# GpSimd makes ten of the 64 drives of a selective scan: steps 11 and 27 join its list

## The reference

```python
x_proj, z = split(x @ W_in + b_in, 2)
u = silu(x_proj)                      # (8, 128, 256)
Bm, Cm = split(u @ W_x + b_x, 2)      # (8, 128, 16) each
dt = softplus(u @ W_dt + b_dt)
def step(h, inp):                     # over the tokens
    u_t, dt_t, B_t, C_t = inp
    dA = exp(dt_t[..., None] * A)
    h = h * dA + (dt_t * u_t)[..., None] * B_t[:, None, :]
    y_t = einsum('bds,bs->bd', h, C_t) + D_param * u_t
    return h, y_t
y = y * silu(z)
```

## Time and profile before

| | us |
|---|---|
| median of 3 runs | 354.48 (354.1 to 355.01) |
| the profiled execution | 354.9 |
| its span in the trace | 353.1 |
| first scan starts | 137.8 |
| last scan starts | 253.2 |

### The profile page before, as it was taken

One profiled execution on the slowest core, in us unless ns is written; L12 is line 12 of the kernel. 1 busy time (PEld: TensorE's weight loads), 2 busy tenths in 40 slices (PEclk: granted clock), 3 DMA queues, 4 the chain that ended last, 5 costly groups with the idle time before them and its releaser, 6 DMA issues.

```text
span 353.1 us, 5637 instructions
## 1 busy us (share of the span) xinstructions
PE 308.1 (87%) x1742; PEld 238.5 (68%) x1742; DVE 294.5 (83%) x743; ACT 215.0 (61%) x504; POOL 196.2 (56%) x233
## 2 busy tenths in 40 slices
PE   8759496898999999599777989898899999999993
PEld 5557395796765566464436865575798779989872
DVE  1898999997987999999999999999949446745945
ACT  4567323334164958667698548888565876756742
POOL 2599996775415062889979898979702800100111
PEclk9958599899999999879999999999999999999998
DMA  7930000000000003565645545536200000000011
GB/s 195 405 161 4 1 0 3 0 1 2 0 2 1 0 0 128 158 186 152 212 144 167 178 130 164 186 124 175 65 2 0 2 0 3 1 0 2 1 32 30
DMA packets 12853, 26.62 MB, mean 75 GB/s; under 512 B 1375, under 2 KB 2527, under 8 KB 12567
## 3 DMA queue, kind: packets, MB, share of 16 engines
q1 hardware_dynamic: 12823, 26.25, 23.2%
HBM read 25.59 MB, written 0.66 MB: 74 GB/s over the span
## 4 chain that ended last, share of the span: by engine, by line
PE 37%; DVE 16%; issue 9%; ACT 7%; POOL 7%; POOLq 0%; DVEq 0%
PE ps L1904 6%; DVE arena L772 5%; DVE ps L759 5%; POOL arena L1117 5%; PE ps L1941 4%; PE ps L1929 4%; PE ps L1930 3%; PE ps L1894 2%; PE ps L1917 2%; PE ps L1918 2%; PE ps L1858 1%; PE ps L1773 1%; PE ps L1592 1%; PE ps L1781 1%; DVE stats L476 1%
## 5 line engine op out<-in xcount | busy, mean ns | idle before, releaser
L1117 POOL TENSOR_TENSOR arena<-arena 128x512 f32<-128x512 f32 x63 | 79.3, 1273 | 21.2 <-DVE arena L772 18.5
L772 DVE TENSOR_TENSOR_SCAN arena<-arena,ps 128x512 f32<-128x512 f32 x56 | 67.0, 1208 | 0.2 <-ACT arena L1394 0.2
L1164 POOL TENSOR_TENSOR rstd<-veps,mhalf 128x4 f32<-128x4 f32 (+2 forms) x6 | 5.0, 838 | 64.4 <-DVE veps L881 35.5
L1394 ACT ACTIVATE arena<-arena,neg_a 128x508 f32<-128x508 f32 x56 | 38.2, 715 | 3.8 <-DVE arena L772 3.4
L800 DVE TENSOR_REDUCE arena<-ps 128x2 f32<-128x496 f32 x32 | 21.3, 666 | 22.6 <-PE ps L1904 22.6
L1858 PE MATMUL ps<-first_in,arena 128*128 128x128 f32 x256 | 39.0, 280 | 0.8 <-POOL arena L1117 0.8
L1858 PEld LDWEIGHTS ps<-first_in,arena 128*128 128x128 f32 x256 | 32.5, 145 | 10.3 <-issue 3.8
L759 DVE TENSOR_TENSOR ps<-arena,ps 128x512 f32<-128x512 f32 x56 | 37.9, 678 | 0.5 <-PE ps L1842 0.4
L1842 PE MATMUL ps<-arena,pick_wide 96*128 96x512 bf16 x56 | 22.0, 398 | 15.2 <-DVE arena L772 13.2
L1671 PE MATMUL ps<-arena,first_in 128*128 128x128 f32 (+1 forms) x192 | 26.7, 303 | 8.6 <-POOL arena L1004 8.6
L1671 PEld LDWEIGHTS ps<-arena,first_in 128*128 128x128 f32 x192 | 25.8, 217 | 11.3 <-POOL arena L1004 11.2
(11 more groups left out here) (291 smaller groups left out, 808.0 us busy)
## 6 DMA issues: line engine op xcount, KB each, us to landing
arena<-bc_rows_dram SPq DMA_DIRECT2D x72, 256.0 KB, 3.3
fold_in<-in_fold_dram SPq DMA_DIRECT2D x1, 2056.0 KB, 12.0
late_in<-in_late_dram SPq DMA_DIRECT2D x1, 1423.5 KB, 17.0
early_in<-in_early_dram SPq DMA_DIRECT2D x1, 921.5 KB, 13.8
xres<-in_x_dram SPq DMA_DIRECT2D x1, 512.0 KB, 14.6
kv_ctx<-in_context_dram SPq DMA_DIRECT2D x1, 480.0 KB, 8.0
rows_in<-in_rows_dram SPq DMA_DIRECT2D x1, 384.0 KB, 14.9
first_in<-in_first_dram SPq DMA_DIRECT2D x1, 320.0 KB, 5.3
```

Of the source, the lines that this page charges most:

```text
L772: nc.vector.tensor_tensor_scan(hist[:, q % NBUF], fade[:, q % NFADE], chain(q), 0.0, ALU.mult, ALU.add).then_inc(S("scan"), 1)
L1117: tt(seen[:, q % NBUF], hist[:, q % NBUF], c_wide[:, q % NBUF], ALU.mult).then_inc(S("read_out"), 1)
L1394: act(decay.rearrange("p (b t) -> p b t", t=T)[:, :, 1:], dt[:, n, cols(g)].rearrange("p (b t) -> p b t", t=T)[:, :, 1:], ACT.Exp, scale=n ...
```

## The change

Two steps are added to the list; nothing else is edited. All that hangs on the list follows from it: for steps 11 and 27 the widening on PE and the drive on DVE go; a memset on DVE, a drive on GpSimd and a broadcast in SP's queue come; the fade goes to PSUM, and its place in `FADES` moves behind the fades of the next two steps.

```diff
-        BY_POOL = (7, 15, 19, 23, 31, 44, 51, 60)
+        BY_POOL = (7, 11, 15, 19, 23, 27, 31, 44, 51, 60)
```

## The result

The changed kernel takes 358.39 us (median of 4 runs, 358.04 to 359.26), beside 354.50 for the kernel before (4 runs, 354.10 to 355.01): 1.0115 times as long, 95% interval 1.0103 to 1.0127; the medians differ by 3.9 us. 358.5 was predicted. The profiled execution took 358.56 us, its span is 356.7; before, 354.9 and 353.1.

The account below looks back on a forecast made before the run. DVE was taken to set the pace of the scan stage. The terms -0.22 + 3.90 + 0.3 gave +4.0 us, so 358.5 us; own range 357.4 to 359.4, with part of Rival 4 357.3 to 360.0.

Parts of the forecast that it names:

- Step 27: ACT, turn 24: fade 29's wait starts the long block 2.69 us later, fade 27 follows it; scan 27 3.90 us late.
- Step 11: Scan 14, held by ACT's softplus waiting for PE, comes 0.22 us earlier through the dropped widening; bounds 0 and 0.95 us.
- The clock: After PE's idle gap behind step 29's widening, half clock slows work towards scan 31: 0.3 us, bounds 0 and 1.0.
- Rival 3: ACT's block delays fade 27, but fade 29 doesn't wait: +1.21 - 0.22, 355.5 us; chance 0.05.
- Rival 1: ACT doesn't hold step 27 back; GpSimd sets the time up to drive 31: 354.1 us; chance 0.06.
- Rival 4: PE at half clock leaves DVE waiting for widened rows over several steps: 1 to 2 us more, about 360; chance 0.12.
- The broadcasts' term of 0: One 256 KB broadcast per added step in SP's queue, ahead of a row of C: 0 taken, bound under 0.5 us.

Follow-up runs that it names:

- the run meant for it: Changed kernel (steps 11 and 27) with fade 27 sent to its SBUF buffer at its ordinary place ahead of ACT's block: 354.97 us.
- the last run: Changed kernel (steps 11 and 27) with added PE matmuls ahead of step 8, in ACT's block at turn 24 and in the gap behind it: 358.38 us.

## Why the prediction was right, and where it was not

**Step 27** was predicted step by step and came so. Fade 29 waited 1.98 us ("about 2") and started 0.04 us behind scan 23's end; from there to fade 27 it is 8.78 us (8.77 predicted); the fade took 0.67 us (0.70), and the scan followed by 0.03. Predicted +3.90, measured 3.88. The runs with fade 27 elsewhere and with the block ahead show that these two causes make it up, 1.18 + 2.70.

**Step 11** had the right sign in the traces, and its term was mis-sized. At full clock its own part is 0.20 us against 0.22, but that is luck, for the 0.22 was reasoned from PE's sequence, and what holds scan 14 there is ACT, whose block starts behind fade 11's wait for the memset. The prediction had that wait (fade 11 at "about 154.1"; 154.11 with PE kept busy) and took it to be covered by 0.84 us that ACT waits for PE later. What the sum left out is that the stretch of PE which it took as given, "shortened only by the widening, 0.22 us", ran at 0.50 of the clock up to 155 us (the widening at 155.23 takes 0.38 us, those from 148.99 to 152.37 take 0.61 to 0.63), and that the clock's return isn't fixed. In the change's execution it came back 1 us earlier, and then the softplus waits for nobody but ACT itself:

```profile
158.19 1.28 ACT L1176 ACT_TABLE_LOAD   x1
...
159.59 0.67 ACT L1381 ACTIVATE arena<-ps,late_in 128x512 f32<-128x512 f32 x1
```

So the gain there was 1.06 us, beyond the bound of 0.95; by the medians of step 11 alone it is 0.40, not clear of noise.

**The clock** term (0.3, bounds 0 and 1.0) had its bounds right, its place only in part, and its 0.3 is no single execution's. In the change's execution it cost nothing at scan 31: fade 31 ended at 195.48, GpSimd's drive at 195.77, and the drive decided. In the run with PE busy in the block it cost 0.92 us from scan 27 on. And in two executions (step 27 alone, PE busy behind step 29) the clock fell inside the block and cost 1.00 us ahead of scan 27, where the prediction had said "inside the block nothing gets slower". That sentence holds only while PE's wait for the softplus leaves the clock up. The Trainium skill (TensorE: Matmul & The Clock Gate, section "What's actually happening") says that idling brings PE to 1.2 GHz and that work releases it; the prediction applied that to the gap alone, and the trace of step 27 alone agrees with it for this wait too (0.50 from 183 to 184 us).

**The rivals.** Rival 3 (355.5) is the run with the block ahead, 355.79. Rival 1 (354.1, GpSimd alone sets the time) could not be seen clean: the run meant for it met the contention in SBUF and gave 354.97. Rival 4 was seen in part: PE at half clock made DVE wait for a widened row, 3.59 us ahead of the drive of step 28 with step 27 alone, but this lay in the gap that fade 27 made anyway. In the run with PE busy in the block its sign came too, DVE waiting for PE by scan 38, at 0.71 us and not the 1 to 2. The broadcasts' term of 0 held, though its bound, under 0.5 us, was given without a row: GpSimd's readouts waited 1.6 us for rows of C in the whole stage, before 2.0, and DVE for none.

**What stays open.** That the total came out at 358.4 against 358.5 is in part luck. The two profiled spans differ by 3.6 us. Of these the two steps make 3.88 - 1.06 = 2.82, where the sum had 4.0 with the clock, and 0.78 is the later start of the stage, which lies ahead of all that the change touches. The medians show more than the traces: step 11 and the change differ by 358.39 - 354.11 = 4.28 us, and by 4.34 with the clock kept up in both; step 27 alone costs 4.48, with 1.00 of the clock's in its profiled execution. The traces give 3.88 for step 27 wherever the clock stays up in the block and behind it. About 0.4 us are thus not accounted for by any one execution that was profiled. They are hardly clear of noise: the interval of the change's ratio alone is 0.4 us wide to either side. And the 4.34 sets runs beside which the kernel before took 354.12 against runs beside which it took 354.46; each against its own, it is 4.26 + 0.42 = 4.68. A low clock ahead of step 8, in the block or behind it isn't the cause in the last run, as far as its one profiled execution shows. Whether anything is left to find, and where, stays open: the start of the stage alone moves by -0.70 to +0.78 us from one profiled execution to another, which is as large as what is sought.

## What to carry to other kernels

When a list reorders work on an in-order engine, write out the new order across each block of other work and look for two things: whose wait now stands last ahead of the block, and whose use now waits for the first instruction behind it. An instruction that leaves the busiest engine is worth its own time (0.57 to 0.59 us here) only at a step where its new engine has room and no block lies between an input's place and its use: step 56 gave 0.5 us, step 27 cost 3.9. A small gain next to an idle stretch of PE is read against a run with PE kept at work, or else the clock's return is taken for the change's merit.

## What the runs showed of the hardware

- One scan with both inputs in SBUF took 1.57 us against 1.21 with one of them in PSUM, and the GpSimd product that met it 2.20 against 1.27.
- PE's clock fell at one idle stretch or another, and not at the same one in each execution of nearly the same program. With step 27 alone it was 1.00 up to 182 us and fell in a wait of 2.15 us for the softplus; the z projection behind it (two matmuls of 128x512) ran at half clock (2.08 us). In the change it was 0.50 already from 178 to 181 us, came back, and the projection behind the same wait, here 1.61 us, ran at full clock (1.12 us). The change's gap of 4.02 us ended at full clock, which fell behind it (0.72 from 191 to 192 us, then 0.50). Six matmuls of 128x256 (2.76 us) in the stretch ahead of step 8 kept the clock at 1.00 there in each of the five kernels that had them.
